# Neighbour search of a two-layer graph kernel: three of four tiles by block maxima of 64 keys, four key buffers, staging on ScalarE

## What is computed

```
h  = relu(layernorm(x))
z  = leaky_relu(lap(adj, h) @ W1 + b1, 0.1)
d2 = |z_i|^2 + |z_j|^2 - 2 z_i . z_j          # 4096 x 4096
S  = exp(-sqrt(max(d2, 0) + 1e-10) / 2)
S  = S where it is among the 4 largest of its row, else 0
x  = x + lap(S + adj, h) @ W2 + b2
h  = relu(layernorm(x))
x  = x + h @ Wself.T + (adj @ h) @ Wneigh.T + b
```

## Time and profile before

| | us |
|---|---|
| median of 3 runs | 1271.79 |
| lowest, highest | 1263.58, 1273.29 |
| the profiled execution | 1267.75 |
| its span, first to last instruction | 1266.1 |
| TensorE, VectorE, ScalarE, GpSimd busy | 971.3, 797.8, 543.0, 610.1 |
| mean granted TensorE clock | 0.902 |

### The profile page before, as it was taken

How to read it: one execution, slowest core, us unless ns; L and a number is a source line. 1 busy time by engine, 2 the same in 40 slices (tenths; PEclk the granted TensorE clock), 3 DMA queues, 4 the chain that set the end, 5 groups by cost and what they waited for, 6 DMA issues and landing times.

```text
span 1266.1 us, 12653 instructions
## 1 busy us (share of the span) xinstructions
PE 971.3 (77%) x3506; PEld 650.9 (51%) x3506; DVE 797.8 (63%) x825; ACT 543.0 (43%) x1089; POOL 610.1 (48%) x913
## 2 busy tenths in 40 slices
PE   0141343654767799989999999479999999899998
PEld 0121122222333354467777777246666667688886
DVE  0946466455355131149999999856655557778885
ACT  0532432443633132145555555434343333677663
POOL 9798787787851000013444444558878874000000
PEclk9975776877887899989999999789999999899999
DMA  9999999999996967168433333589798888599993
GB/s 224 313 356 356 364 358 352 367 358 343 369 369 252 382 238 263 64 185 297 153 149 149 149 149 149 215 281 378 286 351 304 313 306 318 215 363 385 380 383 118
DMA packets 115654, 357.74 MB, mean 283 GB/s; under 512 B 34464, under 2 KB 59808, under 8 KB 87456
## 3 DMA queue, kind: packets, MB, share of 16 engines
q1 hardware_dynamic: 59296, 273.11, 56.8%
q0 software_dynamic: 47104, 80.00, 21.4%
q10 hardware_dynamic: 9216, 4.20, 1.2%
HBM read 250.02 MB, written 106.95 MB: 282 GB/s over the span
## 4 chain that ended last, share of the span: by engine, by line
PE 37%; DMA 20%; DVE 17%; POOL 14%; issue 7%; ACT 2%; SPq 1%; POOLq 1%; ACTq 0%; DVEq 0%
DMA araw<-in_adj_dram 17%; PE ps L1116 7%; POOL araw L361 7%; PE ps L1226 6%; PE ps L1227 6%; PE ps L1228 6%; POOL zt_lo L578 5%; PE ps L1235 4%; DVE m L948 3%; DVE bmax L935 3%; DVE i L950 3%; DVE part L851 2%; PE ps L1205 2%; DVE tr L836 1%; POOL t_st L501 1%
## 5 line engine op out<-in xcount | busy, mean ns | idle before, releaser
L361 POOL DMA_DIRECT2D araw<-in_adj_dram x512 | 302.2, 599 | 62.0 <-ACTq L622 22.4
L1060 DVE TENSOR_TENSOR araw_r<-araw,tr_r 128x2048 fp32r<-128x2048 f32 x96 | 217.8, 2289 | 99.7 <-ACT tr_r L724 71.8
L724 ACT ACTIVATE tr_r<-araw 128x2048 fp32r<-128x2048 f32 x96 | 181.5, 1910 | 85.5 <-DMA araw<-transposed 40.4
L578 POOL DMA_INDIRECT zt_lo<-neighbour_table,idx_st x128 | 175.9, 1374 | 45.8 <-issue 39.8
L699 ACT ACTIVATE araw<-ps,nsq 128x1024 f32<-128x1024 f32 x128 | 142.8, 1117 | 113.2 <-PE ps L1208 94.7
L618 ACT ACTIVATE ps<-araw 128x256 f32<-128x256 f32 x304 | 111.4, 366 | 62.9 <-DMA araw<-in_adj_dram 62.9
L1235 PE MATMUL ps<-araw,ys 128*128 128x512 f32 x256 | 116.9, 600 | 17.6 <-DVE ys L983 17.6
L851 DVE TENSOR_REDUCE part<-araw 128x16 f32<-128x4096 f32 x13 | 57.4, 4414 | 106.2 <-DMA araw<-in_adj_dram 106.2
L1205 PE MATMUL ps<-sq_rows,pick 128*128 128x512 f32 x256 | 102.1, 399 | 17.0 <-POOL zs_lo L489 7.6
L1226 PE MATMUL ps<-araw_r,zt_hi 128*128 128x512 f32 x256 | 101.7, 397 | 3.7 <-DVE araw_r L1060 3.7
L1116 PE MATMUL ps<-araw,ys 128*128 128x512 f32 x224 | 101.3, 602 | 1.5 <-DMA araw<-transposed 1.5
(11 more groups left out here) (153 smaller groups left out, 1658.6 us busy)
## 6 DMA issues: line engine op xcount, KB each, us to landing
araw<-transposed SPq DMA_DIRECT2D x156, 1024.0 KB
araw<-in_adj_dram POOLq DMA_DIRECT2D x512, 128.0 KB, 20.6
keys_scratch<-araw SPq DMA_DIRECT2D x64, 512.0 KB, 4.2
transposed<-tr SPq DMA_DIRECT2D x28, 1024.0 KB, 8.3
transposed<-unit_zt_hi SPq DMA_DIRECT2D x12, 1024.0 KB, 9.1
transposed<-unit_zt_lo SPq DMA_DIRECT2D x12, 1024.0 KB, 9.3
transposed<-unit_sq_rows SPq DMA_DIRECT2D x12, 1024.0 KB, 9.7
xs<-in_x_dram SPq DMA_DIRECT2D x64, 64.0 KB, 2.0
```

The lines of the kernel that those rows point to most:

```text
L361: gp.dma_start(araw[R * q + first:R * q + R:SPREAD, c], adj_v[q, first:R:SPREAD, g // 2, g % 2, :, c]).then_inc(a_first_in[c], DMA)
L578: gp.indirect_dma_start(out=gath[:, i, u, k, :], out_offset=None, in_=table, in_offset=bass.IndirectOffsetOnAxis(ap=idx_st[:, i, u * TOPK ...
L724: act.activation(ring_hi[:, place % TSLOTS], ring[:, j], ACT.Copy).then_inc(hi_done, 1)
L1060: v.tensor_tensor(ring_lo[:, j], ring[:, j], ring_hi[:, place % TSLOTS].bitcast(F32), ALU.subtract).then_inc(lo_done, 1)
```

## The change

Loops run over quads of four tiles. Tiles 0, 1 and 2 of a quad (`VIA = 3`) go by blocks, tile 3 is searched directly. Blocks are 64 keys wide, so there are 64 maxima a lane, and the four gathered blocks are 256 bytes a lane each, 256 candidates. Each of the four tiles has its own key buffer, one for each quarter of `araw`; each of the three block tiles has its own scratch in DRAM and its own candidates' place. `stage_tile` is on ScalarE, right behind `leave` of the tile two before; the first two follow on ScalarE's wait for `nsq`.

VectorE's order in a quad: blocks of tile 0, candidates of tile 2 of the quad before, blocks of 1, blocks of 2, candidates of 0, direct search of 3, candidates of 1. GpSimd's: `read_blocks` of 0, three `keep_top` of the quad before, `read_blocks` of 1, `add_bias` on four tiles, `read_blocks` of 2, `keep_top` of 0. The last `add_bias`, which signals `kept`, stands behind the last `read_blocks` and one `keep_top`.

Since keys fill all of `araw`, SP loads no unit during the search. All eight follow the last `keys_store`, `kept` and the bias load: two each when the stores and maxima of tiles 28, 29 and 30 are done, and the last two when tile 31 is searched. The decoding runs over 96 columns instead of 64, with the block width in place of `F`.

The diff, without declarations and the decoding; from `keys_store` on without the removed lines, which are those of the functions above:

```diff
...
 SLOTS = 4
 TSLOTS = 4
 TOPK = 4
+BLK = 64
+BLOCKS = N // BLK
+QUADS = TILES // 4
+VIA = 3
 SPREAD = 4
 LN_EPS = 1e-5
 DMA = 16
...
-    keys_dram = nc.dram_tensor("keys_scratch", (P * TILES, F), F32).ap()
-    keys_lane = keys_dram.rearrange("(p b) f -> p (b f)", p=P)
+    keys_dram = [nc.dram_tensor(f"keys_scratch{i}", (P * BLOCKS, BLK), F32).ap() for i in range(VIA)]
+    keys_lane = [k.rearrange("(p b) f -> p (b f)", p=P) for k in keys_dram]
...
-        keys = [araw[:, 2 + i].rearrange("p c k -> p (c k)") for i in range(2)]
+        keys = [araw[:, i].rearrange("p c k -> p (c k)") for i in range(4)]
...
-        cand = t_st[:]
-        cand_f = t_st[:].rearrange("p k f -> p (k f)")
+        place_q = place.rearrange("p (i t) k -> p i (t k)", t=VIA)
+        key_place_q = key_place.rearrange("p (i t) k -> p i (t k)", t=VIA)
+        cand_f = [t_st[:, 0:2].rearrange("p k f -> p (k f)"), t_st[:, 2:4].rearrange("p k f -> p (k f)"), out_t[:, 0:TOPK * BLK]]
+        cand = [c.rearrange("p (k f) -> p k f", k=TOPK) for c in cand_f]
...
+            def keys_store(quad, p):
                 for c in range(4):
...
+                    if c == 0 and not (isinstance(quad, int) and quad == 0):
+                        wait_alone(sp, cand_in[p], quad * CAND)
+                    wait_alone(sp, key_ev, quad * 16 + (4 * p + c + 1))
+                    sp.dma_start(keys_lane[p][:, c * 1024:c * 1024 + 1024], keys[p][:, c * 1024:c * 1024 + 1024]).then_inc(keys_out[p], DMA)
+            keys_store(0, 0)
             sp.wait_ge(t_used, USED1)
             for p in range(2):
                 sp.wait_ge(z_out[p], GROUPS // 2 * QD * DMA)
...
             for i in range(UT):
                 sp.wait_ge(at_out[i], STORED[i])
...
+            for p in range(1, VIA):
+                keys_store(0, p)
+            with sp.Fori(1, QUADS) as quad:
+                for p in range(VIA):
+                    keys_store(quad, p)
+            sp.wait_ge(x_b2, QUADS - 1)
             sp.wait_ge(kept, 1)
             sp.dma_start(bias[:], b.partition_broadcast(P)).then_inc(bias_in, DMA)
...
+            for p in range(4):
+                if p < VIA:
+                    sp.wait_ge(keys_out[p], QUADS * 4 * DMA)
+                    sp.wait_ge(block_maxima, (QUADS - 1) * VIA + p + 1)
+                else:
+                    sp.wait_ge(max_done, QUADS)
+                for half in range(CHUNK_UNITS):
+                    load_unit(0, p * CHUNK_UNITS + half)
...
+            def read_blocks(quad, p):
+                if not isinstance(quad, int):
+                    wait_alone(gp, cand_used, quad * VIA + (p - 2))
+                wait_alone(gp, block_places, quad * VIA + (p + 1))
+                gp.tensor_scalar(block_row[:, p], bi8[:, p, 0:TOPK], lane_rows[:, 0:1], None, ALU.add).then_inc(rows_ready, 1)
+                gp.tensor_copy(blocks[:, bass.ds(quad * VIA + p, 1), :].rearrange("p o k -> p (o k)"), bi8[:, p, 0:TOPK]).then_inc(blocks_kept, 1)
+                wait_alone(gp, rows_ready, quad * VIA + (p + 1))
+                wait_alone(gp, keys_out[p], quad * (4 * DMA) + 4 * DMA)
                 for kk in range(TOPK):
                     gp.indirect_dma_start(
...
+                        out=cand[p][:, kk, :], out_offset=None, in_=keys_dram[p],
+                        in_offset=bass.IndirectOffsetOnAxis(ap=block_row[:, p, kk:kk + 1], axis=0),
+                        bounds_check=P * BLOCKS - 1).then_inc(cand_in[p], DMA)
+            def keep_top(quad, p):
+                it = quad * 4 + p
+                if p == VIA:
+                    gp.wait_ge(max_done, quad + 1)
                 else:
...
+                    gp.wait_ge(cand_used, quad * VIA + (p + 1))
+                gp.tensor_copy(vals[:, bass.ds(it, 1), :].rearrange("p o k -> p (o k)"), m8[:, p, 0:TOPK]).then_inc(top_kept[p], 1)
+                gp.tensor_copy(idx[:, bass.ds(it, 1), :].rearrange("p o k -> p (o k)"), i8[:, p, 0:TOPK]).then_inc(top_kept[p], 1)
             load_first(gp)
             for i in range(UT - 2, UT):
...
                 gp.wait_ge(t_used, used_after[last])
             gp.memset(sq_rows[2 * R:P].bitcast(F32), 0.0).then_inc(sq_clear, 1)
             gp.wait_ge(sq_clear, 1)
...
+            def add_bias(quad):
+                four = xs[:, bass.ds(quad * 4, 4), :]
+                return gp.tensor_tensor(four, four, bias[:].unsqueeze(1).broadcast_to([P, 4, F]), ALU.add)
             gp.wait_ge(x_again, X_IN)
             gp.wait_ge(bias_in, 2 * DMA)
...
+            for p in range(VIA):
+                read_blocks(0, p)
+            keep_top(0, 0)
+            with gp.Fori(1, QUADS) as quad:
+                read_blocks(quad, 0)
+                for p in (3, 1, 2):
+                    keep_top(quad - 1, p)
+                read_blocks(quad, 1)
+                add_bias(quad - 1).then_inc(x_b2, 1)
+                read_blocks(quad, 2)
+                keep_top(quad, 0)
+            add_bias(QUADS - 1).then_inc(kept, 1)
+            for p in (3, 1, 2):
+                keep_top(QUADS - 1, p)
...
+            def stage_tile(it, par):
+                dst_h = zs_hi[:, par].rearrange("p (q s) -> p q s", s=R)
+                dst_l = zs_lo[:, par].rearrange("p (q s) -> p q s", s=R)
+                act.activation(dst_h, zt_hi[:, :, bass.ds(it, 1), :].rearrange("p q o s -> p q (o s)"), ACT.Copy).then_inc(zs_ready, 1)
+                act.activation(dst_l, zt_lo[:, :, bass.ds(it, 1), :].rearrange("p q o s -> p q (o s)"), ACT.Copy).then_inc(zs_ready, 1)
+            def leave(quad, p):
+                it = quad * 4 + p
                 for c in range(4):
...
+                    if c == 0 and not (isinstance(quad, int) and quad == 0):
+                        if p < VIA:
+                            act.wait_ge(block_maxima, quad * VIA + (p - 2))
+                            act.wait_ge(keys_out[p], quad * (4 * DMA))
                         else:
...
+                            act.wait_ge(max_done, quad)
                     wait_alone(act, bank_mm, it * 4 + (c + 1))
...
+                    act.activation(keys[p][:, c * 1024:c * 1024 + 1024],
                                    ps[:, 2 * c:2 * c + 2].rearrange("p a b -> p (a b)"), ACT.Identity,
                                    bias=nsq[:, bass.ds(it, 1)], scale=2.0).then_inc(key_ev, 1)
+            def leave_quad(quad, staged):
+                for p in range(4):
+                    leave(quad, p)
+                    if p < staged:
+                        stage_tile(quad * 4 + (p + 2), p % 2)
+            act.wait_ge(zl_done, GROUPS)
+            for par in range(2):
+                stage_tile(par, par)
             act.wait_ge(t_used, USED1)
...
+            leave_quad(0, 4)
+            with act.Fori(1, QUADS - 1) as quad:
+                leave_quad(quad, 4)
+            leave_quad(QUADS - 1, 2)
...
+            link(v.tensor_scalar(lane_rows[:], i8[:, 0, 0:1], float(BLOCKS), None, ALU.mult))
+            def search_blocks(quad, p):
+                key_blocks = keys[p].rearrange("p (b f) -> p b f", f=BLK)
+                if not isinstance(quad, int) or quad * VIA + p > 0:
+                    wait_alone(v, block_places, quad * VIA + p)
+                if isinstance(quad, int) and quad + p == 0:
+                    part_blocks = BLOCKS // 4
                     for c in range(4):
                         v.wait_ge(key_ev, c + 1)
...
+                        ins = v.tensor_reduce(bmax[:, c * part_blocks:(c + 1) * part_blocks], key_blocks[:, c * part_blocks:(c + 1) * part_blocks],
                                               axis=AX_X, op=ALU.max)
                     ins.then_inc(block_maxima, 1)
                 else:
...
+                    wait_alone(v, key_ev, quad * 16 + (4 * p + 4))
                     v.tensor_reduce(bmax[:], key_blocks, axis=AX_X, op=ALU.max).then_inc(block_maxima, 1)
...
+                wait_alone(v, block_maxima, quad * VIA + (p + 1))
                 v.max(bm8[:], bmax[:]).then_inc(best_blocks, 1)
...
+                if not (isinstance(quad, int) and quad == 0):
+                    wait_alone(v, blocks_kept, quad * VIA + (p - 2))
+                wait_alone(v, best_blocks, quad * VIA + (p + 1))
+                v.max_index(bi8[:, p], bm8[:], bmax[:]).then_inc(block_places, 1)
+            def search(quad):
+                if not (isinstance(quad, int) and quad == 0):
+                    wait_alone(v, top_kept[VIA], quad * 2)
+                wait_alone(v, key_ev, quad * 16 + 16)
+                v.max(m8[:, VIA], keys[VIA]).then_inc(chained, 1)
+                wait_alone(v, chained, quad + (count[0] + 1))
+                v.max_index(i8[:, VIA], m8[:, VIA], keys[VIA]).then_inc(max_done, 1)
+            def search_candidates(quad, p):
+                if not isinstance(quad, int) or quad > 0:
+                    wait_alone(v, top_kept[p], quad * 2)
+                wait_alone(v, cand_in[p], quad * CAND + CAND)
```

(25 more changed lines are left out.)

144 lines of the change are left out of this document (23 added, 121 removed).

## The result

| | before | after |
|---|---|---|
| median (lowest to highest), us | 1272.54 (1263.58 to 1273.78) | 1256.94 (1251.97 to 1261.23) |
| the profiled execution, its span | 1267.75, 1266.1 | 1261.23, 1259.3 |

The changed kernel is faster: ratio 0.9891, 95% interval 0.9849 to 0.9932, or 14 us less, give or take 5 (the ratio compares all the times on both sides, not the two medians, which are 15.6 apart). The prediction was 1265.8 with a range of 1253 to 1279: the time is in the range, but on the faster side of 1%, to which I had given 0.29. The two profiled executions differ by 6.5 us only, because that of before was one of its faster ones and that of after its slowest. The same kernel profiled again (`e4_after_again`) has a span of 1253.8.

A forecast was written before the change was run, and what follows sets the result against it. No engine bounds the whole: VectorE, with TensorE close, limits the search, GpSimd's gathers the second stage. Search gain 16.7 less 10.4 given back, taken as -6.0 from median 1271.79, gives 1265.8 us; range 1253 to 1279.

The forecast's parts named there:

- The search becomes TensorE's: Search: TensorE paces four tiles at 29.0 us, VectorE needs 27.5; the search ends 16.7 us sooner.
- The third: Rival, search: 64 outputs make `tensor_reduce` 6.3 us instead of 5.25, so the search gains only 3 us; 1279, chance 0.12.
- the fourth rival: Search: candidates come late and VectorE waits for them, making the kernel slower; 1293, chance 0.12.
- the last candidates be late until 797.0: Search end: tile 30's gathers issue until 793.2 and land late, so the search ends at about 797.0.
- The table is held up by the reload: Behind the search: the table's store waits behind eight unit loads (22.7 us at 369 GB/s) and lands at 830.1.
- the term of 10.4 us given back: Table landing: gathers start 6.3 us sooner, not 16.7, so 10.4 us of the search's gain is lost.
- The gathers' chain: Second stage: a free-running GpSimd chain of 231.6 us from the table's landing sets the stage's end.
- only wait for each other: Second stage: TensorE's -4.3 at worst and the gathers' -6.3 merely wait for each other, so -6 is taken.
- near 1062: Profile sign: the second stage would end near 1062 if the forecast was right.
- 3.4 us on it: Second stage: TensorE's granted clock falls during idle time, 6.8 of 26 us at the lower level, worth 3.4 us.
- 0.3 allowed for TensorE: Sum: the gathers' -6.3 us was taken as -6, because TensorE's path gave -4.3 at worst.
- The second rival: Behind the search: the store isn't held up or GpSimd's chain isn't the bound, so all 16.7 us stay; 1255, chance 0.23.

The follow-up runs named there:

- e4_after_again: The changed kernel word for word, run and profiled again as yardstick: 1255.89 us, ratio 0.9891 to the kernel before.
- e8: The changed kernel with units 0 to 3 loaded right behind the last key stores, units 4 to 7 still behind `kept`: 1250.35 us, ratio 0.9843.
- e5: The changed kernel with the table's store issued by ScalarE's queue instead of SP's: 1261.45 us, ratio 0.9942.
- e9: e8 with the table's store put ahead of the loads of units 4 to 7: 1255.19 us, ratio 0.9890.
- e7b: The kernel before with only three of four neighbours gathered and added in the second stage: 1265.29 us, ratio 0.9958.
- e1: The changed kernel with units 0 to 5 loaded right behind the last key stores, before `kept`: 1251.56 us, ratio 0.9852.
- e3: The changed kernel with blocks of 128 keys, larger candidate places and one added GpSimd wait: 1255.96 us, ratio 0.9888.
- e7a: The changed kernel with only three of four neighbours gathered and added in the second stage: 1246.19 us, ratio 0.9816.

## Why the prediction was right and wrong

- **The search becomes TensorE's.** Right: 32 of 32 us, 29.01 for four tiles against 29.0, the maxima at 4.42, the key evictions of tile 31 done at 784.6 as worked out. The third and the fourth rival are dead: no reduction above 4.5, no wait for candidates. One term was too careful: I let the last candidates be late until 797.0; GpSimd's last issue ended at 792.07 instead of 793.2, they had landed when VectorE came for them, and the search ended at 795.87. With the start of TensorE (0.84 later by its wait for the first staged tile, 1.0 predicted) the gain is 17.9, not 16.7.
- **The table is held up by the reload.** The mechanism is right, by e8 and e5: "however the two share the engines" too, as the table landed no sooner from another queue. The size was off: the term of 10.4 us given back measured 7.5. It was the step that took 369 GB/s from a window of the earlier trace rows whose DMA share was 0.88. The windows above have 428 and 381 GB/s at a share of 1.01. Units and table together took 31.9 us (794.12 to 826.05) instead of 34.5 (the prediction's last line calls that stretch 33 us; by its own terms it is 34.5 from the issue at 795.6, and 35.0 from `kept`). The trace of the kernel before already had the better rate, 30 us further on:

```profile
850.00:855.00 5.00, 5.00 (x18) 3.11 (x17) 1.26 (x1) 1.92 (x1) 3.83 (x4) 1.00 1.02 406
855.00:860.00 5.00, 5.00 (x17) 2.80 (x16) 1.83 (x2) 2.51 (x2) 4.03 (x4) 1.00 1.01 404
```

  With 405 GB/s the eight units come to 20.7 us instead of 22.7, most of what the term was off.
- **The gathers' chain is the bound behind the table.** Right in size, 229.3 to 235.2 us in all profiles with four gathers but e9 (239.5), against 231.6. The reading was too simple, though, and that the size fits is partly luck, since two chains of nearly the same length run side by side. I said the two engines "only wait for each other" and took the gathers for the one that counts. e7b shows TensorE 4 us behind them in the kernel before, and e9 shows TensorE alone setting the end. Over 800 to 1075 us of the chain that ended last, gathers have 46 to 48% in e1, e3 and e5 and 22.5% in the kernel before, but 6% in the changed kernel. There the late table still reaches the end, by another way than I said. The chain in order of time (start, us, what):

```profile
819.38 6.55 DMA neighbour_table<-unit_zt_lo
...
854.05 6.61 DMA zt_lo<-neighbour_table,idx_st
860.75 1.12 DVE out_t L1047 x4
...
871.21 1.90 ACT tr_r L740
873.14 2.31 DVE araw_r L1089
875.49 0.80 PE ps L1255
880.98 1.02 PE ps L1133 x8
...
1060.27 0.91 PE ps L1133 x8
1061.20 1.13 DVE out_t L1047 x4
```

  VectorE stands in the wait for the first gathers, the low parts for TensorE are made later, and from then on TensorE runs at its own pace to the last wait, which is for it. How much of the late table arrives is not settled: against e7a (253.3, no wait) after is 12.0 us later with first waits of 12.4, and e4 6.8 with 6.4, but e5 is 12.9 later with 4.6 and e8 1.3 with 8.5, so the sum of the waits doesn't measure it. The forecast's sign "near 1062" came true (1061.20) because two errors cancel: the table was some 4 us sooner than forecast, and the stretch behind it 3.6 longer; in e4 the last group starts at 1054.26.
- **The clock.** I had put 3.4 us on it in TensorE's path, which the sum then didn't use. It is there, and it varies. Windows of the changed kernel behind the wait of 7.89 us, and the same ones of e4, which had waited 2.46:

```profile
870.00:875.00 5.00, 1.05 (x4) 0.65 (x4) 2.55 (x2) 4.97 (x6) 4.09 (x4) 0.59 0.76 288
875.00:880.00 5.00, 4.51 (x11) 3.55 (x12) 5.00 (x4) 4.47 (x4) 4.39 (x3) 0.50 0.10 27
880.00:885.00 5.00, 5.00 (x19) 3.13 (x18) 2.04 (x1) 0.00 (x0) 3.85 (x4) 0.89 0.59 193
```

```profile
870.00:875.00 5.00, 5.00 (x21) 4.12 (x22) 5.00 (x3) 3.85 (x3) 4.37 (x3) 0.72 0.66 252
875.00:880.00 5.00, 5.00 (x18) 2.60 (x17) 1.30 (x1) 0.00 (x0) 3.58 (x4) 1.00 0.83 262
880.00:885.00 5.00, 5.00 (x22) 3.76 (x23) 4.65 (x17) 0.00 (x0) 3.78 (x5) 1.00 0.62 238
```

In the first TensorE, idle for 4 of 5 us, comes back at the lower level (0.50 is 1.2 GHz), in the second it works at the higher one from 875 on. After's wait is 5.4 us longer, and its last group comes 5.3 us later behind the search. I take the clock as part of that loss and not as a second one; two executions are all there is for it, and no run changes the clock alone. It also falls without such a wait: to 0.66 in 925 to 930 of the kernel before, with TensorE busy for 5.00 of 5 us.

- **The sum.** Predicted: -16.7 + 10.4 + 0.3 = -6.0. By the measured terms -17.9 + 7.5 = -10.4 to the table's landing (826.05 against 836.40). The comparison says -13.8, interval -8.6 to -19. So the gain is more than twice the forecast one, and 4.4 of the 7.8 us between them are the two mis-sized terms (the search 1.2, the reload 2.9) and the 0.3 allowed for TensorE; the other 3.4 lie within the interval, and the profiles don't settle them: they differ by more than that from one execution to the next (229.5 and 235.2 behind the table for the changed kernel, 266.2 and 270.2 in the search for the kernel before). The second rival, that the whole gain stays, came close in time but not in mechanism: 7.5 us are given back at the table's landing, and e8 wins some 6 us, give or take 5 (0.9891 to 0.9843).

## What to carry to other kernels

When a faster stage frees its buffers later, price the reload behind it: what is queued with it, how many bytes pass before the transfer that the next chain waits for, at the rate of a window whose DMA share is 1. Two chains that end within a few us of each other are one bound: lighten each by itself before naming it, and compare the last gather's issue with the end, since the last wait names only who came last. A small wait inside a loop of dependencies costs its length at every turn.

## What was not expected of the hardware

- 1 MiB loads from DRAM moved 428 GB/s for 10 us beside TensorE, VectorE and ScalarE at work; the prediction had gone by a window of 369, and 5 us windows of the kernel before have 404 and 406.
- Loading six units early (e1), while the last candidates were gathered, made VectorE wait 2.31 us for these; with four (e8) it didn't wait.
- The four issues of the table's store took 5.3 us of SP's queue in the kernel before and in e8, but 14.4 in the changed kernel behind eight unit loads, and 15.9 of ScalarE's time in e5. So an issue takes longer while many loads are in flight, and an engine with other work stands for that time; what holds it there isn't shown.
